# A recurrent layer's cell: the tanh of a sum against a sigmoid with a bias, and a reordered cell update

## The chip, the cores and the metric

The kernel runs on one core of one Trainium2 chip. The metric is the device time of one execution in microseconds, the median of several runs; lower is better. The kernel before takes 7336.98 us (median of 3 runs, 7319.33 to 7514.56).

## What is computed

The whole program is a small network over 1250 nodes: a graph layer with attention, a linear-attention mix, a recurrent layer, then a second graph layer, a second attention and two levels of experts. The change touches the recurrent layer alone. It walks over the 1250 nodes as over time steps, with 512 hidden values:

```python
def step(carry, x_t):
    h_prev, c_prev = carry
    combined = jnp.concatenate((x_t, h_prev), axis=1)
    f_t = jax.nn.sigmoid(combined @ W_f + b_f)
    i_t = jax.nn.sigmoid(combined @ W_i + b_i)
    c_tilde = jnp.tanh(combined @ W_c + b_c)
    c_t = f_t * c_prev + i_t * c_tilde
    o_t = jax.nn.sigmoid(combined @ W_o + b_o)
    h_t = o_t * jnp.tanh(c_t)
    return ((h_t, c_t), h_t)
```

Each step needs the hidden state of the step before it, so the 1250 steps are one chain.

## The kernel before, in words

The input's share of the gates is computed for all steps ahead of the loop. In the loop (`lstm`, two steps written out per turn, `par` 0 and 1) TensorE multiplies the hidden state with the recurrent weights. The state is kept in `hp` as two float16 columns, a high part (column 30) and a low part (column 31). The 512 hidden values are 4 columns of 128, and everything after the matmuls is done in two halves `q`: half 0 is columns 0 and 1, half 1 is columns 2 and 3.

TensorE's `rows(par, q, k)` are 16 matmuls of 128 columns: the share of state column `k` in the gates of half `q`. A step has eight of them, 128 matmuls. The first three (48 matmuls) need only state columns 0 and 1 and start at `s_h[0]`. Then TensorE waits for `s_h[1]`, and two more `rows` (32 matmuls) finish the gates of half 0; the last three finish those of half 1. 12 matmuls into `spare` follow, which nothing reads.

VectorE turns the gates of a half to columns (`to_columns`, L1495) and sums the three parts of each (`add_up`, L1501, into `z`). ScalarE takes one tanh over all eight numbers of a half (L1461, into `th`), the gates' sigmoids being written as tanh of half their argument. Column 0 of `th` holds twice the cell. VectorE then forms the two products of the cell (`cell_terms`, L1507, into `terms`: twice the input part, and four times the forget part), opens the output gate (`open_gate`, L1512, into `go`) and sums the cell (`cell_sum`, L1518, back to column 0 of `th`). ScalarE takes the tanh of the cell (L1466, into `tc`), both columns of a half in one instruction. VectorE multiplies it with `go`: once to the float16 high part (`high`, L1525), once to `full` (L1526); `low` (L1531) writes their difference and releases TensorE through `s_h[q]`. ScalarE lays the next step's input (L1454) and keeps the hidden state (L1470) between.

Each engine works through its own list in the order in which it is written here; only semaphores tie them together. The order of a step on VectorE is written out by hand in `step`.

Of the kernel before, what the change touches and what calls it, by code (L numbers as in the profile page):

```python
# [11 lines left out]
ALU = mybir.AluOpType  # L12
ACT = mybir.ActivationFunctionType
# [1298 lines left out]
def lstm(g, d, x, h):  # L1312
# [7 lines left out]
    with ExitStack() as s0:  # L1320
        def sb(name, shape, dt=F32, scope=s0):
            return scope.enter_context(nc.sbuf_tensor(name, shape, dt))
# [3 lines left out]
        scale = sb("l_scale", [P, 2])  # L1326
        h_scale = sb("l_h_scale", [P, 2])
        with ExitStack() as s1:
# [11 lines left out]
            with nc.Block() as block:  # L1340
                @block.gpsimd
                def _(pool):
                    pool.partition_all_reduce(top[:, 1:2], top[:, 0:1], P, RMAX)
# [36 lines left out]
        with ExitStack() as s1:  # L1380
            wx = sb("l_wx", [P, KC, GATES * C], scope=s1)
            bias = sb("l_bias", [P, M16], scope=s1)
# [10 lines left out]
        hp = sb("l_hp", [P, 2, KC, 2 * SPREAD], F16)  # L1393
        turn = sb("l_turn", [P, 2, 2, GATES, 2 * SPREAD])
        z = sb("l_z", [P, 2, 8])
        th = sb("l_th", [P, KC, GATES + 1])
        terms = sb("l_terms", [P, KC, 2])
        go = sb("l_go", [P, KC])
        tc = sb("l_tc", [P, KC])
        full = sb("l_full", [P, 2, KC])  # L1400
        half_h = sb("l_half_h", [P, 2])
# [4 lines left out]
        def pair(name):  # L1406
            return [s0.enter_context(g.semaphore(f"l_{name}{q}")) for q in range(2)]

        s_gates, s_turned, s_sum, s_tanh, s_terms, s_open, s_cell, s_tcell, s_full, s_h = [
            pair(n) for n in ("gates", "turned", "sum", "tanh", "terms", "open", "cell", "tcell", "full", "h")]  # L1410
# [37 lines left out]

        @block.scalar
        def _(act):  # L1450
            act.preload_act_table(ACT.Tanh)

            def lay_input(t, par):
                act.activation(turn[:, par, :, :, 0:34:33].rearrange("p q g v -> p q v g"),  # L1454
                               xp[:, bass.ds(t, 1), :].rearrange("p a (q v g) -> p (a q) v g", q=2, v=2),
                               ACT.Copy).then_inc(s_input, 1)

            def step(t, par):
                for q in range(2):
                    act.wait_ge(s_sum[q], t + 1)  # L1460
                    act.activation(th[:, 2 * q:2 * q + 2, 1:],  # L1461
                                   z[:, q, :].rearrange("p (j m) -> p j m", m=GATES), ACT.Tanh,
                                   scale=2.0 ** -Z_BITS).then_inc(s_tanh[q], 1)
                for q in range(2):
                    act.wait_ge(s_cell[q], t + 1)
                    act.activation(tc[:, 2 * q:2 * q + 2], th[:, 2 * q:2 * q + 2, 0], ACT.Tanh,  # L1466
                                   scale=0.5).then_inc(s_tcell[q], 1)
                lay_input(t + 1, 1 - par)
                act.wait_ge(s_full[1], t + 1)
                act.activation(h[:, :, bass.ds(t, 1)].rearrange("p j a -> p (j a)"), full[:, par, :],  # L1470
                               ACT.Copy).then_inc(s_kept, 1)
            act.wait_ge(s_clean, 1)
            lay_input(0, 0)
            with act.Fori(0, N, 2) as t:
                step(t, 0)
                step(t + 1, 1)

        @block.vector
        def _(dve):
            for par in range(2):  # L1480
                for q in range(2):
                    dve.memset(banks[par][q][:, :], 0.0)
            for u in range(2):
                g.link(dve, dve.tensor_copy(half_h[:, u:u + 1], h_scale[:, 0:1]))
            g.link(dve, dve.memset(th[:, :, :], 0.0))
            dve.memset(turn[:, :, :, :, :], 0.0).then_inc(s_clean, 1)  # L1486
            g.link(dve, dve.memset(hp[:, 1, :, :], 0.0))
            dve.memset(hp[:, 0, 0:2, :], 0.0).then_inc(s_h[0], 1)
            dve.memset(hp[:, 0, 2:4, :], 0.0).then_inc(s_h[1], 1)

            def to_columns(t, par, q):
                dve.wait_ge(s_gates[q], t + 1)
                if q == 0:
                    dve.wait_ge(s_input, t + 1)
                dve.transpose(turn[:, par, q, :, 1:33],  # L1495
                              banks[par][q][:, 0:128].rearrange("p (m r) -> p m r", r=32)).then_inc(s_turned[q], 1)

            def add_up(t, par, q):
                dve.wait_ge(s_turned[q], t + 1)
                three = turn[:, par, q, :, :].rearrange("p g (v e) -> p v g e", e=SPREAD)[:, :, :, 0:3]  # L1500
                dve.tensor_reduce(z[:, q, :].rearrange("p (v g) -> p v g", g=GATES), three, AX.X,  # L1501
                                  ALU.add).then_inc(s_sum[q], 1)

            def cell_terms(t, q):
                two = slice(2 * q, 2 * q + 2)
                dve.wait_ge(s_tanh[q], t + 1)
                dve.scalar_tensor_tensor(terms[:, two, :], th[:, two, 1:3], 1.0, th[:, two, 0:GATES + 1:GATES],  # L1507
                                         ALU.add, ALU.mult).then_inc(s_terms[q], 1)

            def open_gate(t, q):  # L1510
                two = slice(2 * q, 2 * q + 2)
                dve.scalar_tensor_tensor(go[:, two], th[:, two, 3], 1.0, half_h[:, :], ALU.add,  # L1512
                                         ALU.mult).then_inc(s_open[q], 1)

            def cell_sum(t, q):
                two = slice(2 * q, 2 * q + 2)
                dve.wait_ge(s_terms[q], t + 1)
                dve.scalar_tensor_tensor(th[:, two, 0], terms[:, two, 0], 0.5, terms[:, two, 1], ALU.mult,  # L1518
                                         ALU.add).then_inc(s_cell[q], 1)

            def high(t, par, q):
                two = slice(2 * q, 2 * q + 2)
                dve.wait_ge(s_tcell[q], t + 1)
                dve.wait_ge(s_open[q], t + 1)
                dve.tensor_tensor(hp[:, 1 - par, two, 30], go[:, two], tc[:, two], ALU.mult)  # L1525
                dve.tensor_tensor(full[:, par, two], go[:, two], tc[:, two], ALU.mult).then_inc(s_full[q], 1)  # L1526

            def low(t, par, q):
                two = slice(2 * q, 2 * q + 2)
                dve.wait_ge(s_full[q], t + 1)  # L1530
                dve.tensor_tensor(hp[:, 1 - par, two, 31], full[:, par, two], hp[:, 1 - par, two, 30],  # L1531
                                  ALU.subtract).then_inc(s_h[q], 1)

            def step(t, par):
                to_columns(t, par, 0)
                add_up(t, par, 0)
                to_columns(t, par, 1)
                cell_terms(t, 0)
                open_gate(t, 0)
                add_up(t, par, 1)  # L1540
                cell_sum(t, 0)
                cell_terms(t, 1)
                high(t, par, 0)
                cell_sum(t, 1)
                low(t, par, 0)
                open_gate(t, 1)
                high(t, par, 1)
                low(t, par, 1)
            with dve.Fori(0, N, 2) as t:
                step(t, 0)  # L1550
                step(t + 1, 1)
            dve.wait_ge(s_h[1], N + 1)
            dve.wait_ge(s_kept, N)
            dve.scalar_tensor_tensor(x[:, :, 0:N], h[:, :, 0:N], h_scale[:, 1:2], x[:, :, 0:N], ALU.mult, ALU.add)
# [516 lines left out]
```

## Time and profile before

| | us |
|---|---|
| median of 3 runs | 7336.98 |
| profiled execution | 7332.33 |
| its span | 7330.6 |
| stretch of the recurrent loop (first to last `low` of the trace) | 1965.7 to 6229.5 |
| TensorE busy in the whole span | 5252.2 (72%) |
| VectorE busy | 3870.4 (53%) |
| ScalarE busy | 1844.6 (25%) |

The loop takes more than half of the span. The engines' shares over the whole span say little, since the parts outside the loop have other limits. In the loop the same pattern of instructions comes 1250 times, with the same gaps, so one step in the order of time tells what the others do. The columns of each view are named in the section of rows.

### The profile page before, as it was taken

The numbers are of one execution on the slowest core, as the hardware profiler recorded it, in microseconds if no ns is written. First come the engines' busy times: TensorE is split into PE (matmuls) and PEld (weight loads), VectorE is DVE, ScalarE is ACT, GpSimd is POOL, SyncE is SP. The second block draws the span as 40 slices with busy tenths as digits, with TensorE's granted clock in tenths as the row PEclk, the third lists the DMA queues.
The fourth block names the chain that finished last, engine by engine and source line by source line (L and its number), as shares of the span: only waits on it lengthen the run. The fifth ranks groups of instructions, "written<-read, shape, count | busy, mean of one in ns | idle before, by whom it ended". The sixth has DMA issues, their size and how long they took to land. (4 is left out here: it accounts for less than half of the span.)

```text
span 7330.6 us, 411790 instructions
## 1 busy us (share of the span) xinstructions
PE 5252.2 (72%) x180989; PEld 3541.9 (48%) x180989; DVE 3870.4 (53%) x22246; ACT 1844.6 (25%) x8790; POOL 875.2 (12%) x891
## 2 busy tenths in 40 slices
PE   1256354775977777777777777777777777877799
PEld 1122122442555555555555555555555555553445
DVE  6115355733466666666666666666666666573112
ACT  1001004820033333333333333333333333200011
POOL 0717563500000000000000000000000000350000
PEclk7677677987999999999999999999999999997899
DMA  2116465511000000000000000000000000230100
GB/s 71 40 70 200 138 175 100 159 37 46 0 0 0 0 0 0 0 0 0 0 0 0 0 0 0 0 0 0 0 0 0 0 0 0 86 80 23 46 0 15
DMA packets 116203, 235.83 MB, mean 32 GB/s; under 512 B 65390, under 2 KB 67054, under 8 KB 112251
## 3 DMA queue, kind: packets, MB, share of 16 engines
q0 software_dynamic: 56032, 162.48, 7.9%
q1 hardware_dynamic: 60058, 72.02, 3.2%
q8 instruction: 51, 0.84, 0.0%
q14 instruction: 62, 0.50, 0.0%
HBM read 219.99 MB, written 14.45 MB: 32 GB/s over the span
## 5 line engine op out<-in xcount | busy, mean ns | idle before, releaser
L1422 PE MATMUL l_bank<-l_w,l_hp 128*32 128x128 f16 x160000 | 2464.4, 219 | 998.7 <-DVE l_hp L1531 993.6
L1422 PEld LDWEIGHTS l_bank<-l_w,l_hp 128*32 128x32 f16 x160000 | 2246.3, 97 | 1633.0 <-DVE l_hp L1531 1627.4
L1495 DVE STREAM_TRANSPOSE l_turn<-l_bank 128x128 f32<-128x128 f32 x2500 | 794.5, 318 | 1180.0 <-PE l_bank L1422 1005.6
L1461 ACT ACTIVATE l_th<-l_z 128x8 f32<-128x8 f32 x2500 | 523.3, 209 | 2127.1 <-DVE l_z L1501 2127.1
L1443 PE MATMUL l_spare<-l_w 128*2 128x512 f16 x15000 | 1025.7, 379 | 0.0
L1674 POOL DMA_INDIRECT ga_rows<-r_table,dst_t x176 | 168.0, 955 | 4643.7 <-DMA r_table<-c_r 4516.4
L1466 ACT ACTIVATE l_tc<-l_th 128x2 f32<-128x2 f32 x2500 | 490.9, 196 | 464.3 <-DVE l_th L1518 464.3
L1507 DVE SCALAR_TENSOR_TENSOR l_terms<-l_th 128x4 f32<-128x4 f32 x2500 | 359.2, 144 | 256.1 <-ACT l_th L1461 256.1
L1525 DVE TENSOR_TENSOR l_hp<-l_go,l_tc 128x2 f16<-128x2 f32 x2500 | 422.0, 169 | 130.4
L1501 DVE TENSOR_REDUCE l_z<-l_turn 128x8 f32<-128x24 f32 x2500 | 447.2, 179 | 42.6
L1531 DVE TENSOR_TENSOR l_hp<-l_full,l_hp 128x2 f16<-128x2 f32 x2500 | 422.2, 169 | 43.2
L1518 DVE SCALAR_TENSOR_TENSOR l_th<-l_terms 128x2 f32<-128x2 f32 x2500 | 386.0, 154 | 0.0
L1526 DVE TENSOR_TENSOR l_full<-l_go,l_tc 128x2 f32<-128x2 f32 x2500 | 385.6, 154 | 0.0
L1512 DVE SCALAR_TENSOR_TENSOR l_go<-l_th,l_half_h 128x2 f32<-128x2 f32 x2500 | 381.6, 153 | 0.0
L1443 PEld LDWEIGHTS l_spare<-l_w 128*2 128x2 f16 x15000 | 304.6, 84 | 152.4
L1470 ACT ACTIVATE xn<-l_full 128x4 f32 x1250 | 262.3, 210 | 359.8 <-DVE l_full L1526 359.8
L1137 PE MATMUL at_bank<-at_rows,at_onehot 128*128 128x512 f32 x352 | 199.8, 650 | 124.5 <-ACT at_rows L1096 54.1
L1454 ACT ACTIVATE l_turn<-l_xp 128x16 f32 (+1 forms) x1251 | 275.0, 220 | 2.6 <-DVE l_turn L1486 2.6
L751 POOL DMA_INDIRECT sm_q_rows<-q_table,sorted_e x176 | 199.4, 1133 | 275.1 <-POOLq L117 140.1
L1960 PE MATMUL e_y<-e_hid,e_w 128*128 128x512 f32 (+1 forms) x576 | 222.1, 541 | 0.0
L913 DVE TENSOR_TENSOR sm_q_rows<-sm_q_rows,sm_k_rows 128x512 f32<-128x512 f32 x176 | 122.1, 694 | 187.7 <-DMA sm_k_rows<-k_table,sorted_e 179.5
L1989 DVE TENSOR_TENSOR e_masked<-e_h,e_m_all 128x512 f32<-128x512 f32 (+1 forms) x72 | 40.0, 597 | 324.5 <-PE e_h L1945 324.5
(413 smaller groups left out, 4896.0 us busy)
## 6 DMA issues: line engine op xcount, KB each, us to landing
keys<-in_src_by_tile SPq DMA_DIRECT2D x7, 1344.0 KB
e_w<-in_e_W SPq DMA_DIRECT2D x2, 4096.0 KB
w<-in_g_W SPq DMA_DIRECT2D x2, 2048.0 KB, 10.4
l_wh<-in_l_Wh SPq DMA_DIRECT2D x1, 4096.0 KB
l_wx<-in_l_Wx SPq DMA_DIRECT2D x1, 4096.0 KB
e_w<-in_e_W SPq DMA_DIRECT2D x2, 2048.0 KB
sm_q_rows<-q_table,sorted_e POOLq DMA_INDIRECT x176
sm_k_rows<-k_table,sorted_e POOLq DMA_INDIRECT x176
```

The lines of the kernel that those rows point to most:

```text
L1422: mm = pe.matmul(banks[par][q][32 * j:32 * j + 32, 0:128], hp[:, par, k, 30 - 30 * v:62 - 30 * v], w16[:, part, k, j, 256 * q + 128 * v:25 ...
L1443: pe.matmul(spare[32 * j:32 * j + 2, 0:512], w16[:, 0, k, j, 0:2], w16[:, 0, k, j, :], start=True, stop=True)
L1461: act.activation(th[:, 2 * q:2 * q + 2, 1:], z[:, q, :].rearrange("p (j m) -> p j m", m=GATES), ACT.Tanh, scale=2.0 ** -Z_BITS).then_inc(s ...
L1466: act.activation(tc[:, 2 * q:2 * q + 2], th[:, 2 * q:2 * q + 2, 0], ACT.Tanh, scale=0.5).then_inc(s_tcell[q], 1)
L1495: dve.transpose(turn[:, par, q, :, 1:33], banks[par][q][:, 0:128].rearrange("p (m r) -> p m r", r=32)).then_inc(s_turned[q], 1)
L1501: dve.tensor_reduce(z[:, q, :].rearrange("p (v g) -> p v g", g=GATES), three, AX.X, ALU.add).then_inc(s_sum[q], 1)
L1507: dve.scalar_tensor_tensor(terms[:, two, :], th[:, two, 1:3], 1.0, th[:, two, 0:GATES + 1:GATES], ALU.add, ALU.mult).then_inc(s_terms[q], 1)
L1512: dve.scalar_tensor_tensor(go[:, two], th[:, two, 3], 1.0, half_h[:, :], ALU.add, ALU.mult).then_inc(s_open[q], 1)
L1518: dve.scalar_tensor_tensor(th[:, two, 0], terms[:, two, 0], 0.5, terms[:, two, 1], ALU.mult, ALU.add).then_inc(s_cell[q], 1)
L1525: dve.tensor_tensor(hp[:, 1 - par, two, 30], go[:, two], tc[:, two], ALU.mult)
L1526: dve.tensor_tensor(full[:, par, two], go[:, two], tc[:, two], ALU.mult).then_inc(s_full[q], 1)
L1531: dve.tensor_tensor(hp[:, 1 - par, two, 31], full[:, par, two], hp[:, 1 - par, two, 30], ALU.subtract).then_inc(s_h[q], 1)
```

## The change

The cell's tanh is written as a sigmoid: tanh(c) = 2 (sigmoid(2c) - 0.5). ScalarE's activation computes a function of scale times the input plus a bias, and a bias can be a column of memory, one number per partition. So the sum of the two products moves into the activation: with `terms[:, j, 0]` as input, scale 0.5 and `terms[:, j, 1]` as bias, ScalarE needs no `cell_sum` ahead of it. The bias is one number per partition, so each of the four columns takes an instruction of its own; there were two instructions per step, one per half, and there are four. `high` now subtracts 0.5 in the same instruction that multiplies with `go` (`scalar_tensor_tensor` in place of `tensor_tensor`), and `half_h` is doubled once ahead of the loop. `cell_sum` stays, because the next step needs the cell, but nothing in the same step waits for it; instead `cell_terms` waits for `s_cell` of the step before. Two small memsets ahead of the loop give `s_cell` its first count. The table of functions that ScalarE loads ahead of the loop is asked for by Sigmoid instead of Tanh.

Two orders change. On ScalarE both tanh of the gates stood ahead of both tanh of the cell; now each half's cell operations stand right behind its gates. On VectorE `high(0)` goes ahead of `cell_terms(1)`, and `cell_sum(1)` goes behind `open_gate(1)`.

```diff
-            act.preload_act_table(ACT.Tanh)
+            act.preload_act_table(ACT.Sigmoid)
...
-                for q in range(2):
-                    act.wait_ge(s_cell[q], t + 1)
-                    act.activation(tc[:, 2 * q:2 * q + 2], th[:, 2 * q:2 * q + 2, 0], ACT.Tanh,
-                                   scale=0.5).then_inc(s_tcell[q], 1)
+                    act.wait_ge(s_terms[q], t + 1)
+                    for j in (2 * q, 2 * q + 1):
+                        ins = act.activation(tc[:, j:j + 1], terms[:, j, 0:1], ACT.Sigmoid, scale=0.5,
+                                             bias=terms[:, j, 1:2])
+                    ins.then_inc(s_tcell[q], 1)
...
-                g.link(dve, dve.tensor_copy(half_h[:, u:u + 1], h_scale[:, 0:1]))
+                g.link(dve, dve.tensor_scalar(half_h[:, u:u + 1], h_scale[:, 0:1], 2.0, None, ALU.mult))
...
+            for q in range(2):
+                dve.memset(th[:, 2 * q:2 * q + 2, 0], 0.0).then_inc(s_cell[q], 1)
...
                 dve.wait_ge(s_tanh[q], t + 1)
+                dve.wait_ge(s_cell[q], t + 1)
...
-                dve.tensor_tensor(hp[:, 1 - par, two, 30], go[:, two], tc[:, two], ALU.mult)
-                dve.tensor_tensor(full[:, par, two], go[:, two], tc[:, two], ALU.mult).then_inc(s_full[q], 1)
+                dve.scalar_tensor_tensor(hp[:, 1 - par, two, 30], tc[:, two], 0.5, go[:, two], ALU.subtract, ALU.mult)
+                dve.scalar_tensor_tensor(full[:, par, two], tc[:, two], 0.5, go[:, two], ALU.subtract,
+                                         ALU.mult).then_inc(s_full[q], 1)
...
                 cell_sum(t, 0)
+                high(t, par, 0)
                 cell_terms(t, 1)
-                high(t, par, 0)
-                cell_sum(t, 1)
                 low(t, par, 0)
                 open_gate(t, 1)
+                cell_sum(t, 1)
                 high(t, par, 1)
```

ScalarE's list for one step of the kernel before, from the gates of the loop's first step on; `l_th<-l_z` is the tanh of a half's gates, `l_tc<-l_th` that of its cell:

```order
L1461 ACTIVATE l_th<-l_z 128x2x4 x2
L1466 ACTIVATE l_tc<-l_th 128x2 x2
L1454 ISA
L1454 ACTIVATE l_turn<-l_xp 128x2x2x4
L1470 ISA
L1470 ACTIVATE xn<-l_full 128x4
```

The same step on ScalarE in the changed kernel:

```order
L1461 ACTIVATE l_th<-l_z 128x2x4
L1466 ACTIVATE l_tc<-l_terms 128x1 x2
L1461 ACTIVATE l_th<-l_z 128x2x4
L1466 ACTIVATE l_tc<-l_terms 128x1 x2
L1454 ISA
L1454 ACTIVATE l_turn<-l_xp 128x2x2x4
L1471 ISA
L1471 ACTIVATE xn<-l_full 128x4
```

The two instructions of half 0's cell now stand between the two tanh of the gates, each reads one column, and no load of another table stands in the loop.

VectorE's list before, from the second `add_up` of a step to its last `low`:

```order
L1501 TENSOR_REDUCE l_z<-l_turn 128x8
L1518 SCALAR_TENSOR_TENSOR l_th<-l_terms 128x2
L1507 SCALAR_TENSOR_TENSOR l_terms<-l_th 128x4
L1525 TENSOR_TENSOR l_hp<-l_go,l_tc 128x2
L1526 TENSOR_TENSOR l_full<-l_go,l_tc 128x2
L1518 SCALAR_TENSOR_TENSOR l_th<-l_terms 128x2
L1531 TENSOR_TENSOR l_hp<-l_full,l_hp 128x2
L1512 SCALAR_TENSOR_TENSOR l_go<-l_th,l_half_h 128x2
L1525 TENSOR_TENSOR l_hp<-l_go,l_tc 128x2
L1526 TENSOR_TENSOR l_full<-l_go,l_tc 128x2
L1531 TENSOR_TENSOR l_hp<-l_full,l_hp 128x2
```

And in the changed kernel, where each line number of these functions is 3 to 5 higher:

```order
L1504 TENSOR_REDUCE l_z<-l_turn 128x8
L1522 SCALAR_TENSOR_TENSOR l_th<-l_terms 128x2
L1529 SCALAR_TENSOR_TENSOR l_hp<-l_tc,l_go 128x2
L1530 SCALAR_TENSOR_TENSOR l_full<-l_tc,l_go 128x2
L1511 SCALAR_TENSOR_TENSOR l_terms<-l_th 128x4
L1536 TENSOR_TENSOR l_hp<-l_full,l_hp 128x2
L1516 SCALAR_TENSOR_TENSOR l_go<-l_th,l_half_h 128x2
L1522 SCALAR_TENSOR_TENSOR l_th<-l_terms 128x2
L1529 SCALAR_TENSOR_TENSOR l_hp<-l_tc,l_go 128x2
L1530 SCALAR_TENSOR_TENSOR l_full<-l_tc,l_go 128x2
L1536 TENSOR_TENSOR l_hp<-l_full,l_hp 128x2
```

`high` of half 0 (two instructions) has moved ahead of the second `cell_terms`, and the second `cell_sum` has moved behind `low(0)` and `open_gate(1)`. The list has as many instructions as before.

## Rows read from the trace of the kernel before

**Rows 1.** Busy time by stage: stretch, length, PE, PEld, DVE, ACT, POOL, PEclk, DMA share, GB/s.
```profile
3000.00:4000.00 1000.00, 767.03 (x41020) 582.60 (x41020) 613.17 (x4688) 308.88 (x1758) 0.00 (x0) 1.00 0.00 0
```

**Rows 2.** The line of `low`: count, ns min/median/max, first and last start.
```profile
L1531 DVE TENSOR_TENSOR l_hp<-l_full,l_hp x2500: 168/169/171, 1965.7 to 6229.5; 128x2 f16<-128x2 f32 x193
```

**Rows 3.** Timeline of one step: start us, duration us, engine, line, out<-in, [idle before].
```profile
4001.62 0.32 DVE L1495 STREAM_TRANSPOSE l_turn<-l_bank 128x128 f32<-128x128 f32 x1 [0.81 <-PE l_bank L1422]
4001.97 0.18 DVE L1501 TENSOR_REDUCE l_z<-l_turn 128x8 f32<-128x24 f32 x1
...
4002.18 0.21 ACT L1461 ACTIVATE l_th<-l_z 128x8 f32<-128x8 f32 x1 [1.24 <-DVE l_z L1501]
4002.29 0.32 DVE L1495 STREAM_TRANSPOSE l_turn<-l_bank 128x128 f32<-128x128 f32 x1
4002.53 0.12 DVE L1507 SCALAR_TENSOR_TENSOR l_terms<-l_th 128x4 f32<-128x4 f32 x1
...
4002.64 0.18 DVE L1501 TENSOR_REDUCE l_z<-l_turn 128x8 f32<-128x24 f32 x1
4002.74 0.15 DVE L1518 SCALAR_TENSOR_TENSOR l_th<-l_terms 128x2 f32<-128x2 f32 x1
4002.85 0.21 ACT L1461 ACTIVATE l_th<-l_z 128x8 f32<-128x8 f32 x1 [0.46 <-DVE l_z L1501]
4002.97 0.19 ACT L1466 ACTIVATE l_tc<-l_th 128x2 f32<-128x2 f32 x1
4003.09 0.16 DVE L1507 SCALAR_TENSOR_TENSOR l_terms<-l_th 128x4 f32<-128x4 f32 x1 [0.21 <-ACT l_th L1461]
4003.19 0.17 DVE L1525 TENSOR_TENSOR l_hp<-l_go,l_tc 128x2 f16<-128x2 f32 x1
4003.26 0.15 DVE L1526 TENSOR_TENSOR l_full<-l_go,l_tc 128x2 f32<-128x2 f32 x1
4003.34 0.16 DVE L1518 SCALAR_TENSOR_TENSOR l_th<-l_terms 128x2 f32<-128x2 f32 x1
4003.45 0.17 DVE L1531 TENSOR_TENSOR l_hp<-l_full,l_hp 128x2 f16<-128x2 f32 x1
4003.53 0.20 ACT L1466 ACTIVATE l_tc<-l_th 128x2 f32<-128x2 f32 x1 [0.37 <-DVE l_th L1518]
...
4003.68 1.79 PEld L1422 LDWEIGHTS l_bank<-l_w,l_hp 128*32 128x32 f16 x128 [1.30 <-DVE l_hp L1531]
4003.68 1.97 PE L1422 MATMUL l_bank<-l_w,l_hp 128*32 128x128 f16 x128 [0.80 <-DVE l_hp L1531]
4003.79 0.17 DVE L1525 TENSOR_TENSOR l_hp<-l_go,l_tc 128x2 f16<-128x2 f32 x1
...
4004.06 0.17 DVE L1531 TENSOR_TENSOR l_hp<-l_full,l_hp 128x2 f16<-128x2 f32 x1
...
4005.03 0.32 DVE L1495 STREAM_TRANSPOSE l_turn<-l_bank 128x128 f32<-128x128 f32 x1 [0.80 <-PE l_bank L1422]
```

**Rows 4.** Groups of ScalarE with an operand of one number per partition: count, busy, mean ns.
```profile
L1096 ACT ACTIVATE at_rows<-at_rows,weight_t 128x64 f32<-128x64 f32 x528 | 144.5, 336 | 24.9 <-DMA at_rows<-v_table,dst_t 21.3 <-issue 0.7
...
L1084 ACT ACTIVATE at_apart<-numbers_f,at_minus_lo 128x128 f32<-128x128 f32 x176 | 68.0, 386 | 41.6 <-DVE at_minus_lo L1104 41.3 <-PE at_bank L1138 0.3
```

**Rows 5.** Timeline of ScalarE: three such instructions back to back.
```profile
1300.25 0.81 ACT L1096 ACTIVATE at_rows<-at_rows,weight_t 128x64 f32<-128x64 f32 x3
```

**Rows 6.** Timeline of the loop's first step, in which TensorE has its lower clock.
```profile
1961.00 3.49 PE L1422 MATMUL l_bank<-l_w,l_hp 128*32 128x128 f16 x128 [5.19 <-DVE l_hp L1488]
1963.38 0.32 DVE L1495 STREAM_TRANSPOSE l_turn<-l_bank 128x128 f32<-128x128 f32 x1 [2.36 <-PE l_bank L1422]
```

**Rows 7.** Stretch of that first step, TensorE's gate matmuls (L1422) alone; columns as in the view by stage.
```profile
1961.00:1964.00 3.00, 3.00 (x116) 3.00 (x120) 0.50 0.00 0
```

**Rows 8.** Groups of ScalarE: the load of a function table.
```profile
L1451 ACT ACT_TABLE_LOAD x1 | 1.3, 1283 | 208.8 <-PEq L73 208.8
```

## The prediction, made before the changed kernel was run

> **What bounds the kernel now.** I read the busy time by stage first: in a stretch inside the recurrent loop TensorE is busy 77% of the time, VectorE 61%, ScalarE 31%, no DMA moves, and TensorE's granted clock is 1.00, which is 2.4 GHz [rows 1]. No engine is full, so a chain of latencies sets the time. The line of `low` gives the period: 2500 instructions, two per step, the first starting at 1965.7 and the last at 6229.5 us; 4263.8 us over 1249.5 steps is 3.41 us per step [rows 2]. 0.01 us per step is therefore 12.5 us of the kernel, and everything is decided in the timeline of one step [rows 3].
>
> I set the first transpose (half 0, 4001.62) to zero; the next comes at 4005.03, 3.41 later. In that chain an engine starts about 0.03 us after the one that releases it has ended (sum of half 1 ends 4002.82, its tanh starts 4002.85; `cell_sum(1)` ends 4003.50, its tanh starts 4003.53), and VectorE behind ScalarE takes 0.03 to 0.06 (tanh of the cell 1 ends at 4003.73, `high(1)` starts 4003.79) [rows 3].
>
> Two chains go round, one for each half of the state.
> - Half 0: sum, tanh of gates, terms, `cell_sum(0)` ends at 1.27, its tanh runs 1.35 to 1.54, `high`, `full`, `low(0)` 1.83 to 2.00, TensorE starts at 2.06. From there to the next transpose 1.35. Sum 3.41: this is the chain that binds.
> - Half 1: tanh of gates ends 1.44, `cell_terms(1)` 1.47, `cell_sum(1)` 1.72 to 1.88 (behind `high` and `full` of half 0 on VectorE, not at its earliest), tanh of the cell 1.91 to 2.11, `high(1)` 2.17, `low(1)` 2.44 to 2.61. Adding the same 0.06, TensorE can see it at 2.67.
>
> When does TensorE want half 1? Its 128 weight loads span 1.79 us, the last of them taking some 0.09, so they start 13.4 ns apart [rows 3]. The 49th, the first that needs half 1, starts 48 x 13.4 = 0.64 after 2.06, at 2.70. Half 1 is there at 2.67. **The second half is hidden by 0.03 us, no more.** That is the number to watch: whatever makes half 0 faster is capped there, and whatever makes half 1 later than 0.03 us is paid in full.
>
> The return of half 1 is shorter than that of half 0 only because 48 matmuls are done already: 1.35 - 0.64 = 0.71 from the 49th to the transpose. As a check, 2.67 + 0.71 = 3.38, against the 3.41 of half 0.
>
> **The change, part by part.**
>
> Removed from the path: `cell_sum` ahead of each tanh of the cell. In half 0 the terms end at 1.03 (4002.65) and the cell operation can start at 1.06, where the tanh of the cell started at 1.35: 0.29 earlier. (Of this, `cell_sum(0)` cost only 0.15; the rest was its place behind the second sum, and the tanh of half 1's gates on ScalarE.)
>
> Added: each cell operation is two instructions with a bias column. The old one took 0.19 to 0.20 for both columns [rows 3]. The loop has none with a column operand; the rest of the program has. 128x128 elements with a bias column take 386 ns, 128x64 with a scale column 336 [rows 4]. The 64 elements between them cost about 50, so a width of one leaves about 280 ns. Three of the 64-wide ones back to back take 0.81 us [rows 5]; (0.81 - 0.336) / 2 = 0.237 from start to start, less 0.05 for the width: 0.19. A pair then takes s = 0.19 + 0.28 = 0.47 us from first start to end, against 0.20: **+0.27 each, twice in a step**. The bounds: if the column cost nothing at this width, a pair takes 0.10 + 0.195 = 0.295 (0.12 from tanh start to tanh start at 8 elements [rows 3]); if the two did not overlap at all, 0.56. I take 0.47, because both forms of rows 4 give the same base of 280.
>
> Half 0 after: cell operation 1.06 to 1.53; `high(0)` 1.56, `full` 1.64, `low(0)` at about 1.83, where it was. The 0.29 gained by the missing sum and the earlier place are spent on 0.27 of longer pair and a little waiting: half 0 breaks even.
>
> Half 1 after: ScalarE is held by the pair until 1.44 (1.06 + 2 x 0.19), so the tanh of half 1's gates, ready at 1.23, runs 1.44 to 1.65 instead of 1.23 to 1.44. On VectorE `cell_terms(1)` now stands behind `high(0)` and `full`: 1.64 + 0.08 = 1.72 at the earliest, and 1.68 by the tanh. It sits exactly where `cell_sum(1)` was (1.72), so the delayed tanh costs nothing and the removed sum gains nothing: in half 1 `terms` has only taken its place. Then comes the long pair. In general, with s: pair 0 ends 1.06 + s; `high(0)` +0.03; `full` +0.075; `cell_terms(1)` +0.075, ends +0.155; pair 1 starts +0.03, ends +s; `high(1)` +0.06; `low(1)` +0.27, ends +0.17; TensorE +0.06; transpose +0.71. **Period = 2.70 + 2s.** With s = 0.47 that is 3.64, and +0.23 per step. The stall shows between the 48th and the 49th matmul.
>
> Costed at nothing: `scalar_tensor_tensor` for `tensor_tensor` (both kinds on 128x2 take 0.15 with a float32 result [rows 3], and I give the float16 one its old 0.17); `cell_sum(0)`, in VectorE's pause before `high(0)`; `cell_sum(1)` and `open_gate(1)`, in its pause before `high(1)`, now about 0.5 us long (uncovered they would be 0.15 each); the wait for `s_cell`, given a step before (queued behind it are `low(0)` and all that follows, so 0.03 for a second wait would be passed on: it is in the range). The input laid for the next step ends about 0.27 later than before, at some 2.8, against the transpose at 3.64. The three instructions ahead of the loop are a fraction of a microsecond.
>
> Sum: 1250 x 0.23 = 288 us on the profiled execution's 7332.33, which lies 5 us under the median of the runs: **7620 us**, 3.9% slower.
>
> A table of functions is also asked for by Sigmoid. One load takes 1283 ns [rows 8]. If each change between tanh and sigmoid needed one, a step would take four, 5.1 us or more, some 6400 us in all. The changed program's list shows none inside the loop, so I leave this out. The Trainium skill (ScalarE: Activation LUTs, Table sets) says that functions come in sets and that sigmoid's set has tanh too. By that there is nothing to pay either; before a run no row shows it.
>
> **The rivals.**
> - The column costs little on a width of one (s = 0.295). Then the period is 3.29 by the formula, and half 0 gives 2.93 + s (1.06, +0.03 to `high`, +0.26 and +0.17 through `low`, +0.06, +1.35), 3.23. Saving 0.12 x 1250 = 150: 7180 us. For it: no instruction this narrow with a column operand is in the trace. Against: two widths, one base. It decides below s = 0.355, where 2.70 + 2s is 3.41. The two-per-cent line towards slower (+147 us, 0.117 per step) is at s = 0.41. Chance 0.07.
> - Half 1 is hidden after all, since TensorE's loads run ahead of what I read, or the waits behind `high` are shorter. Half 0 sets the period, 3.41 to 3.45: 7332 to 7380 us, no change to be measured. Against: the check 3.38 against 3.41 leaves no room for 0.2. Chance 0.06.
> - TensorE's clock falls, as its pauses grow by 0.23 us per step. The first step ran at a granted clock of 0.50, 1.2 GHz [rows 7], and took 2.38 from its start to the transpose against 1.35 [rows 6]. +1.03 per step would be 8900 us. For it: that step followed 5 us of idle. Against: two pauses of 0.8 and 0.23 with matmuls between, and 12 spare ones. Chance 0.02.
> - A longer step, same mechanism: no overlap in the pair, s = 0.56, period 3.82, 7845 us. Chance 0.04, of which the range leaves out most.
>
> **How the numbers follow.** The forecast's mechanism (half 1 late by twice the longer pair, less the 0.29 gained and the 0.03 hidden) has 0.81; its own range is +0.17 to +0.30 per step (s from 0.44 to 0.49, and 0.02 to 0.03 of second waits), 7540 to 7710. Reaching towards the rivals on both sides, 7500 to 7730 for 8 in 10. A difference of 2% is about what a measurement of this kernel can tell. Faster by more than that needs s under 0.30: 0.04. Within it, the rest of the first two rivals and the low tail of the forecast: 0.10. Slower: 0.86.
>
> **What would show it.** The cell operations: 2500 become 5000, about 0.28 each, starts 0.19 apart. `cell_sum` ends nobody's wait; ScalarE's pause before the second cell operation is ended by `l_terms`. TensorE's 128 matmuls split into 48 and 80 with a pause of about 0.2 between, released by `low(1)`, while half 0's `low` comes, from the first transpose, no later than before. Period 3.64. I am wrong if the pair takes under 0.41, if the 48 and 80 stay one block, or if half 0's `low` has moved by more than 0.05 either way.

## The result, and the profile after

| | before | after |
|---|---|---|
| median of the runs, us | 7335.96 (4 runs) | 7578.09 (4 runs) |
| profiled execution, us | 7332.33 | 7561.06 |
| first and last `low` of the loop, us | 1965.7, 6229.5 | 1959.0, 6463.3 |
| one step (the difference over 1249.5) | 3.412 | 3.605 |

The changed kernel is slower: ratio 1.0335, 95% interval 1.0307 to 1.0362. One of the four runs of the kernel before took 7514.56 us, over 2% more than the other three, and the ratio leaves it out. One step became 0.193 us longer, and 1250 x 0.193 is 241 us; the medians differ by 242. Everything outside the loop is as it was (the profiled execution differs by 229, because its loop began 7 us earlier and what follows took 5 us less).

The two lines that answer to [rows 2] and [rows 1] in the trace of after: first the line of `low`, with the starts of its first and last instruction; then a stretch inside the loop, with busy time of PE, PEld, DVE, ACT, POOL, then the granted clock.

```profile
L1536 DVE TENSOR_TENSOR l_hp<-l_full,l_hp x2500: 168/168/170, 1959.0 to 6463.3; 128x2 f16<-128x2 f32 x193
```

```profile
3000.00:4000.00 1000.00, 776.51 (x38791) 553.86 (x38780) 573.05 (x4443) 444.55 (x2220) 0.00 (x0) 1.00 0.00 0
```

ScalarE went from 309 to 445 us busy in 1000, with the clock of TensorE at 1.00 as before. VectorE's share fell, since the same work is spread over a longer step. The groups of the page show the new instruction and what waits on it (busy, mean ns, then the idle time ahead of it):

```profile
L1466 ACT ACTIVATE l_tc<-l_terms 128x1 f32<-128x1 f32 x5000 | 1202.7, 287 | 707.3 <-DVE l_terms L1511 707.3
...
L1529 DVE SCALAR_TENSOR_TENSOR l_hp<-l_tc,l_go 128x2 f16<-128x2 f32 x2500 | 420.7, 168 | 740.2 <-ACT l_tc L1466 740.2
```

`high` (now L1529) waits 740 us in all for the cell operation, 0.30 per half. Before, the idle time ahead of `high` was 130 us with no such release named.

One step of after in the timeline, to be laid beside [rows 3]; the first transpose is at 4001.56:

```profile
4001.56 0.32 DVE L1498 STREAM_TRANSPOSE l_turn<-l_bank 128x128 f32<-128x128 f32 x1 [0.74 <-PE l_bank L1422]
...
4002.47 0.12 DVE L1511 SCALAR_TENSOR_TENSOR l_terms<-l_th 128x4 f32<-128x4 f32 x1
...
4002.63 0.48 ACT L1466 ACTIVATE l_tc<-l_terms 128x1 f32<-128x1 f32 x2 [0.29 <-DVE l_terms L1511]
...
4003.01 0.19 ACT L1461 ACTIVATE l_th<-l_z 128x8 f32<-128x8 f32 x1
4003.14 0.17 DVE L1529 SCALAR_TENSOR_TENSOR l_hp<-l_tc,l_go 128x2 f16<-128x2 f32 x1 [0.31 <-ACT l_tc L1466]
4003.22 0.16 DVE L1530 SCALAR_TENSOR_TENSOR l_full<-l_tc,l_go 128x2 f32<-128x2 f32 x1
4003.29 0.16 DVE L1511 SCALAR_TENSOR_TENSOR l_terms<-l_th 128x4 f32<-128x4 f32 x1
4003.41 0.17 DVE L1536 TENSOR_TENSOR l_hp<-l_full,l_hp 128x2 f16<-128x2 f32 x1
4003.48 0.48 ACT L1466 ACTIVATE l_tc<-l_terms 128x1 f32<-128x1 f32 x2 [0.27 <-DVE l_terms L1511]
...
4003.63 0.68 PEld L1422 LDWEIGHTS l_bank<-l_w,l_hp 128*32 128x32 f16 x48 [1.31 <-DVE l_hp L1536]
...
4003.99 0.17 DVE L1529 SCALAR_TENSOR_TENSOR l_hp<-l_tc,l_go 128x2 f16<-128x2 f32 x1 [0.28 <-ACT l_tc L1466]
...
4004.26 0.17 DVE L1536 TENSOR_TENSOR l_hp<-l_full,l_hp 128x2 f16<-128x2 f32 x1
...
4004.48 1.13 PEld L1422 LDWEIGHTS l_bank<-l_w,l_hp 128*32 128x32 f16 x80 [0.17 <-DVE l_hp L1536]
4005.16 0.32 DVE L1498 STREAM_TRANSPOSE l_turn<-l_bank 128x128 f32<-128x128 f32 x1 [0.74 <-PE l_bank L1422]
```

Two things are to be seen. `low` of half 0 starts 1.85 us after the first transpose, where it started 1.83 before: half 0 has won nothing and lost next to nothing. And TensorE's block of 128 weight loads has broken in two, 48 and 80, with a pause of 0.17 us that ends with `low` of half 1. Before, `low` of half 1 started at 2.44 from the first transpose; now it starts at 2.70.

### The profile page after: what moved, and what is told of

Its sections match the earlier page's. It is cut to its first block and busy times, and to the rows that moved or that the text cites. A ratio compares the mean times of both kernels' runs of the same rounds, so it can differ in the third digit from the quotient of the medians.

```text
span 7559.3 us, 416792 instructions
## 1 busy us (share of the span) xinstructions
PE 5488.1 (73%) x180989; PEld 3556.8 (47%) x180989; DVE 3835.5 (51%) x22248; ACT 2528.1 (33%) x11290; POOL 878.4 (12%) x891
## 5 line engine op out<-in xcount | busy, mean ns | idle before, releaser
L1422 PE MATMUL l_bank<-l_w,l_hp 128*32 128x128 f16 x160000 | 2694.0, 220 | 1009.5 <-DVE l_hp L1536 1003.6
L1422 PEld LDWEIGHTS l_bank<-l_w,l_hp 128*32 128x32 f16 x160000 | 2259.3, 97 | 1860.4 <-DVE l_hp L1536 1854.8
L1466 ACT ACTIVATE l_tc<-l_terms 128x1 f32<-128x1 f32 x5000 | 1202.7, 287 | 707.3 <-DVE l_terms L1511 707.3
L1461 ACT ACTIVATE l_th<-l_z 128x8 f32<-128x8 f32 x2500 | 504.1, 202 | 1469.3 <-DVE l_z L1504 1469.3
L1529 DVE SCALAR_TENSOR_TENSOR l_hp<-l_tc,l_go 128x2 f16<-128x2 f32 x2500 | 420.7, 168 | 740.2 <-ACT l_tc L1466 740.2
L1530 DVE SCALAR_TENSOR_TENSOR l_full<-l_tc,l_go 128x2 f32<-128x2 f32 x2500 | 384.7, 154 | 0.0
```

The lines of the kernel that those rows point to most:

```text
L1422: mm = pe.matmul(banks[par][q][32 * j:32 * j + 32, 0:128], hp[:, par, k, 30 - 30 * v:62 - 30 * v], w16[:, part, k, j, 256 * q + 128 * v:25 ...
L1461: act.activation(th[:, 2 * q:2 * q + 2, 1:], z[:, q, :].rearrange("p (j m) -> p j m", m=GATES), ACT.Tanh, scale=2.0 ** -Z_BITS).then_inc(s ...
L1466: ins = act.activation(tc[:, j:j + 1], terms[:, j, 0:1], ACT.Sigmoid, scale=0.5, bias=terms[:, j, 1:2])
L1529: dve.scalar_tensor_tensor(hp[:, 1 - par, two, 30], tc[:, two], 0.5, go[:, two], ALU.subtract, ALU.mult)
L1530: dve.scalar_tensor_tensor(full[:, par, two], tc[:, two], 0.5, go[:, two], ALU.subtract, ALU.mult).then_inc(s_full[q], 1)
```

## The experiments

In all of them I read the step's length from the first and last start of `low`. Five of them ran on two other chips, on which the kernel before takes 7128 and 7122 us (last column of the table); on the first of these, the four kernels and the one before were run once each. The loop begins there some 190 us sooner (`low` first starts at 1768.8 us with a third instruction in half 0, at 1959.0 in after), while the loop itself is no different as far as these runs show: with that third instruction the time is 478.5 us over before's on the same chip, and 1250 x (3.791 - 3.412) is 474. So the step is the measure, and times are compared with before on the same chip. Times in the steps' accounts are from the first transpose. "Pair" is the two instructions of a half's cell operation, and s is the time from its first start to its end: 0.48 us in after.

| kernel | step, us | against before | time, us | before there |
|---|---|---|---|---|
| before | 3.412 | | 7335.96 | |
| after | 3.605 | +0.193 | 7578.09 | 7335.96 |
| one instruction, no bias | 3.144 | -0.268 | 6803.73 | 7127.88 |
| two instructions, no bias | 3.235 | -0.177 | 6898.29 | 7127.88 |
| a third one in half 0 | 3.791 | +0.379 | 7606.42 | 7127.88 |
| a third one in half 1 | 3.792 | +0.380 | 7600.12 | 7127.88 |
| changed cell in half 0 only | 3.527 | +0.115 | 7485.68 | 7341.08 |
| changed cell in half 1 only | 3.412 | 0.000 | 7341.21 | 7341.08 |
| both orders alone | 3.556 | +0.144 | 7518.31 | 7341.08 |
| changed cell, old orders | 3.689 | +0.277 | 7472.48 | 7121.54 |
| after, TensorE's rows early | 3.585 | +0.173 | 7558.26 | 7341.08 |

### How long is the pair, and why

```diff
-                    for j in (2 * q, 2 * q + 1):
-                        ins = act.activation(tc[:, j:j + 1], terms[:, j, 0:1], ACT.Sigmoid, scale=0.5,
-                                             bias=terms[:, j, 1:2])
-                    ins.then_inc(s_tcell[q], 1)
+                    act.activation(tc[:, 2 * q:2 * q + 2], terms[:, 2 * q:2 * q + 2, 0], ACT.Sigmoid,
+                                   scale=0.5).then_inc(s_tcell[q], 1)
```

> The changed kernel, but each half's cell operation is one sigmoid over both columns of the first product, with no bias; the second product is left out of the sigmoid, so this kernel computes another hidden state. The pair (0.48 us from first start to end in the trace of after) becomes one instruction of about 0.20. Theory 1 (the length of the pair, once per half in one chain, is the whole price; after's own trace gives period = 2.64 + 2s): the formula gives 3.04, but then half 0 and TensorE's 48 matmuls set it, at about 3.15 us per step instead of 3.61, some 7000 us in all, faster than before too; TensorE's weight loads are one block of 128 again. Theory 2 (the new orders on ScalarE and VectorE, or the second waits, cost the time): the step stays above 3.41 us, 7330 us or more.

Measured: 3.144 us per step. The line of the cell operation and TensorE's loads in its trace:

```profile
L1465 ACT ACTIVATE l_tc<-l_terms x2500: 203/203/204, 1774.0 to 5702.0; 128x2 f32<-128x2 f32 x193
```

```profile
4004.10 1.80 PEld L1422 LDWEIGHTS l_bank<-l_w,l_hp 128*32 128x32 f16 x128 [1.03 <-DVE l_hp L1534]
```

With the same orders, the same second waits and the same instructions on VectorE, but an operation of 0.20 us instead of a pair of 0.48, the loop is 0.27 us per step shorter than before, and the block of loads is whole. So the new orders and the second waits don't keep the step above 3.41 once the pair is short, and theory 2 falls. The terms of half 0, which have one of the new waits, start 0.91 us after the first transpose in before and in after alike (4002.53 and 4002.47). What the orders cost where the sum stays is another matter, and is measured below.

```diff
-                        ins = act.activation(tc[:, j:j + 1], terms[:, j, 0:1], ACT.Sigmoid, scale=0.5,
-                                             bias=terms[:, j, 1:2])
+                        ins = act.activation(tc[:, j:j + 1], terms[:, j, 0:1], ACT.Sigmoid, scale=0.5)
```

> As the run before, but still two instructions per half, one per column, each without the bias column (the second product is left out of the sigmoid here too). This parts the price of a second instruction from that of the column operand. If the column operand is what makes the pair long (0.09 per instruction), a pair takes 0.30: period 3.24 us by the formula 2.64 + 2s, 7105 us. If it is the second instruction as such, whatever its operands, the pair stays near 0.48 and the kernel at 7560 us.

Measured: 3.235 us per step, and this line (count, ns min/median/max):

```profile
L1466 ACT ACTIVATE l_tc<-l_terms x5000: 186/195/203, 1762.7 to 5805.4; 128x1 f32<-128x1 f32 x193
```

```profile
4002.08 0.29 ACT L1466 ACTIVATE l_tc<-l_terms 128x1 f32<-128x1 f32 x2 [0.29 <-DVE l_terms L1510]
```

Without the column operand an instruction takes 195 ns, with it 287, both on one column; a pair takes 0.29 against 0.48. The second instruction costs 0.09 us and the two column operands together 0.19. The Trainium skill (ScalarE: Activation LUTs, What ACT_TABLE_LOAD costs) gives some 93 ns for each such operand and as much for the overlap of two activations in a row; the 92 ns here and the starts 0.19 apart agree.

### Are both pairs in the chain?

A third sigmoid with a bias column goes into a spare column, in half 0 or in half 1:

```diff
                     for j in (2 * q, 2 * q + 1):
+                        if j == 1:
+                            act.activation(tc[:, KC:KC + 1], terms[:, j - 1, 0:1], ACT.Sigmoid, scale=0.5,
+                                           bias=terms[:, j - 1, 1:2])
```

> The changed kernel with one more sigmoid with a bias column (into a spare column that nothing reads) between the two of half 0 only. The group of half 0 grows from 0.48 to 0.67 us. Theory 1 (half 0's pair delays half 1 through VectorE's order: high and full of half 0 stand ahead of the terms of half 1): +0.19 us per step, 3.80, 7800 us. Theory 2 (only half 1's pair is on the path, half 0 has slack while TensorE waits for half 1): no change, 7560 us.

> The same third instruction in half 1 only. Theory 1: also +0.19 us per step, 3.80, 7800 us, with TensorE's pause between its 48th and 49th weight load grown from 0.17 to 0.36. Theory 2, were half 0 the one that binds: less than that, the more so the more half 1 is covered.

Measured: 3.791 and 3.792, +0.186 and +0.187 over after, for 0.19 us more in one half. Of half 0 it is plain why in the trace: `high` goes from 1.58 to 1.77 (4002.20, the first transpose being at 4000.43), the terms of half 1 behind it from 1.73 to 1.92. In half 1 it shows in TensorE's pause between 48 and 80 loads, 0.36 us against 0.17:

```profile
4003.96 0.68 PEld L1422 LDWEIGHTS l_bank<-l_w,l_hp 128*32 128x32 f16 x48 [1.32 <-DVE l_hp L1539]
4005.00 1.13 PEld L1422 LDWEIGHTS l_bank<-l_w,l_hp 128*32 128x32 f16 x80 [0.36 <-DVE l_hp L1539]
```

So the step grows by s of each half, 2s in all, once half 1 is late. The slack of half 0 towards TensorE doesn't help: half 1's terms stand behind half 0's `high` in VectorE's list.

### One half at a time

The changed operation in half 0 only, with the changed orders, except that the sum of half 1 stands ahead of `open_gate(1)` and not behind it (half 1 keeps its sum and its one tanh; `half_h` has a value for each column):

```diff
+NEW = 0
...
+                if q == NEW:
+                    act.wait_ge(s_terms[q], t + 1)
+                    for j in (2 * q, 2 * q + 1):
+                        ins = act.activation(tc[:, j:j + 1], terms[:, j, 0:1], ACT.Sigmoid, scale=0.5,
+                                             bias=terms[:, j, 1:2])
+                    ins.then_inc(s_tcell[q], 1)
+                else:
+                    act.wait_ge(s_cell[q], t + 1)
+                    act.activation(tc[:, 2 * q:2 * q + 2], th[:, 2 * q:2 * q + 2, 0], ACT.Tanh,
+                                   scale=0.5).then_inc(s_tcell[q], 1)
```

> Half 0 has the changed cell operation and the changed orders; half 1 has the old one (cell sum, then one tanh over both columns), with its cell sum right behind low of half 0. Theory 1, worked out on after's timeline: terms of half 1 end at 1.89 from the first transpose, cell sum 1.93 to 2.08, tanh 2.11 to 2.31, high 2.35, low ends 2.79, TensorE 2.84, transpose at 3.52: +0.11 us per step against before, 7470 us, ratio 1.019 to before. Theory 2 (each pair costs its own 0.27, the sum it replaces is worth little): about half of the whole loss, 7450 us; the two are not told apart by this run but by the next.

Measured: 7485.68 us, ratio 1.020 (1.0183 to 1.0217), 3.527 us per step. As said there, this one alone decides nothing. The same with `NEW = 1`, and both orders as in the kernel before:

> Half 1 has the changed cell operation, half 0 the old one, and both engines' orders are those of before. Theory 1 (what matters is where the terms of half 1 stand): they can start at 1.47, behind the tanh of the gates and ahead of high of half 0, the pair runs 1.66 to 2.14, high of half 1 at 2.17 where it was before; half 0 still binds: 3.41 us per step, 7335 us, the same as before within 0.3%. Theory 2 (a pair costs 0.27 wherever it stands): +0.25 us per step, or at least half of the change's loss, 7450 us or more.

Measured: 7341.21 us, ratio 0.9997 (0.9987 to 1.0006), 3.412 us per step. The pair is in its trace, 0.48 us long, and costs nothing:

```profile
4002.00 0.16 DVE L1522 SCALAR_TENSOR_TENSOR l_terms<-l_th 128x4 f32<-128x4 f32 x1 [0.21 <-ACT l_th L1474]
4002.09 0.17 DVE L1546 TENSOR_TENSOR l_hp<-l_go,l_tc 128x2 f16<-128x2 f32 x1
...
4002.20 0.48 ACT L1463 ACTIVATE l_tc<-l_terms 128x1 f32<-128x1 f32 x2
...
4002.71 0.17 DVE L1541 SCALAR_TENSOR_TENSOR l_hp<-l_tc,l_go 128x2 f16<-128x2 f32 x1
```

The first transpose is at 4000.52 here. The terms of half 1 start at 1.48, ahead of half 0's `high`, the pair runs from 1.68 to 2.16, and half 1's `high` starts at 2.19, against 2.17 in the kernel before. The sum that was taken away stood late on VectorE, at 1.72 behind `high` and `full` [rows 3]; without it the pair starts 0.23 earlier and is 0.28 longer. A pair is not a loss in itself. It is one where it can't start earlier by about as much as it is longer.

### The orders alone, and the operation alone

The kernel before with the changed orders and nothing else:

```diff
-                for q in range(2):
                     act.wait_ge(s_cell[q], t + 1)
                     act.activation(tc[:, 2 * q:2 * q + 2], th[:, 2 * q:2 * q + 2, 0], ACT.Tanh,
                                    scale=0.5).then_inc(s_tcell[q], 1)
...
-                cell_terms(t, 1)
                 high(t, par, 0)
-                cell_sum(t, 1)
+                cell_terms(t, 1)
                 low(t, par, 0)
                 open_gate(t, 1)
+                cell_sum(t, 1)
```

> The kernel before with both orders of the change (ScalarE: each half's cell tanh behind its gates; VectorE: high of half 0 ahead of the terms of half 1, cell sum of half 1 behind open gate) and nothing else of it: the sum and the one tanh per half stay. Theory 1: half 1's terms wait until 1.68, its sum until 1.94, TensorE sees it at 2.85: 3.53 us per step, +0.12, 7480 us. A rival (the orders are harmless, the pair alone is the loss): 7335 us.

Measured: 7518.31 us, ratio 1.0237 (1.022 to 1.0254), +0.144 per step, 0.02 more than expected. Three lines of its timeline, the first transpose being at 4001.65: the terms of half 1 start at 1.69 (1.47 in before), its sum at 1.96 (1.72), its tanh at 2.14.

```profile
4003.34 0.16 DVE L1506 SCALAR_TENSOR_TENSOR l_terms<-l_th 128x4 f32<-128x4 f32 x1
...
4003.61 0.15 DVE L1517 SCALAR_TENSOR_TENSOR l_th<-l_terms 128x2 f32<-128x2 f32 x1
...
4003.79 0.20 ACT L1465 ACTIVATE l_tc<-l_th 128x2 f32<-128x2 f32 x1 [0.54 <-DVE l_th L1517]
```

And the changed operation in both halves with the old orders:

```diff
-                    act.wait_ge(s_terms[q], t + 1)
-                    for j in (2 * q, 2 * q + 1):
+                for q in range(2):
+                    act.wait_ge(s_terms[q], t + 1)
+                    for j in (2 * q, 2 * q + 1):
...
-                high(t, par, 0)
                 cell_terms(t, 1)
+                high(t, par, 0)
+                cell_sum(t, 1)
                 low(t, par, 0)
                 open_gate(t, 1)
-                cell_sum(t, 1)
```

> The other half of the cut made by the run of the orders alone: the new cell operation in both halves, with both engines' orders as before (both tanh of the gates ahead of both pairs; terms of half 1 ahead of high of half 0). The two pairs then follow each other on ScalarE: 1.35 to 1.83 and 1.73 to 2.21 from the first transpose, high of half 0 at 1.86, its low ends 2.29, TensorE 2.35, and half 0 binds: 3.70 us per step, +0.29 against before, 7700 us, ratio 1.049, with TensorE's loads in one block of 128 (half 1 follows 0.4 us behind half 0 and is hidden). If the losses simply add (both +0.193, orders alone +0.144), the operation alone would be +0.05, 7400 us.

Measured: 7472.48 us, ratio 1.0486 (1.0468 to 1.0503), 3.689 us per step, +0.277. ScalarE does its four instructions in one row, 0.84 us, and TensorE's loads are whole: half 0 binds here.

```profile
4000.26 0.84 ACT L1467 ACTIVATE l_tc<-l_terms 128x1 f32<-128x1 f32 x4
...
4000.76 0.17 DVE L1530 SCALAR_TENSOR_TENSOR l_hp<-l_tc,l_go 128x2 f16<-128x2 f32 x1 [0.21 <-ACT l_tc L1467]
...
4001.25 1.80 PEld L1422 LDWEIGHTS l_bank<-l_w,l_hp 128*32 128x32 f16 x128 [1.58 <-DVE l_hp L1537]
```

Orders alone +0.144, operation alone +0.277, both together +0.193: the parts don't add. With the old orders half 0's pair starts behind the second tanh of the gates and half 0 pays; with the new ones half 0 is even and half 1 pays. The new orders take 0.08 off what the new operation costs, but nothing off the kernel before.

### Filling the pause

```diff
                 rows(par, 1, 0, first=True)
+                rows(par, 1, 1)
                 pe.wait_ge(s_h[1], t + 1)
                 rows(par, 0, 2)
                 rows(par, 0, 3, signal=s_gates[0])
-                rows(par, 1, 1)
```

> The changed kernel, and TensorE does the 16 matmuls of state column 1 for half 1's gates ahead of its wait for half 1 of the state instead of behind half 0's gates. They fill the pause (0.85 us from half 0 to half 1, 64 matmuls take 0.86). Theory 1: the first transpose is not earlier for it, since half 1's arrival sets it, but the gates of half 1 are ready 0.21 us earlier, the second transpose no longer holds the terms of half 0 back (0.91 becomes about 0.81 from the first transpose): -0.09 us per step, 3.51, 7450 us. If the second transpose doesn't hold the terms: no change, 7560 to 7578 us.

Measured: 7558.26 us, 3.585 us per step, 0.02 less than after where I had expected 0.09. The mechanism is there but small, and it meets the next limit. From its timeline, the first transpose being at 4000.19:

```profile
4000.64 0.32 DVE L1498 STREAM_TRANSPOSE l_turn<-l_bank 128x128 f32<-128x128 f32 x1
4001.00 0.17 DVE L1511 SCALAR_TENSOR_TENSOR l_terms<-l_th 128x4 f32<-128x4 f32 x1
```

The second transpose comes at 0.45 instead of 0.67 and the terms start at 0.81 instead of 0.91. But here they take 0.17 us instead of 0.12, so they end only 0.05 earlier. Half 1's `low` starts at 2.65, as much earlier as that. And TensorE's pause is gone: it starts at 2.01, and 96 matmuls stand between that and the first transpose, 1.57 us, 0.22 more than the 1.35 of 80 [rows 3]. Half 0 binds again at 2.01 + 1.57 = 3.58, with half 1 right at its heels: `low(1)` ends at 2.82, and the load of the 65th matmul, the first that needs half 1, starts 0.855 after the first load, at 2.87, where it starts 0.852 behind the first in before.

No kernel that computes the whole layer was faster than the one before. The one without the second product (3.144) shows what a cheap sum inside the activation would be worth, not a way to it.

## Why the prediction was right, and where its sizes were off

It said 7620 us, range 7500 to 7730, slower; measured were 7578. By its own steps:

- **The chain and its slack.** Right. Half 1 was hidden by no more than 0.03: in the run with the pair in half 1 only it came 0.02 later and nothing moved, and in after it came 0.26 later (`low(1)` 2.44 to 2.70) and the step grew by 0.193. Of the 0.26, some 0.03 were hidden and 0.04 came back behind TensorE's pause (see the formula below).
- **The length of the pair.** Predicted 0.47 from instructions 64 and 128 wide, measured 0.48; 287 ns each against 280. The rows themselves gave 286 (336 less 50), which I had rounded down. The rival of a cheap column at a width of one is out: 195 ns without the column, 287 with it.
- **Half 0 breaks even.** Right: `low(0)` at 1.85 against 1.83.
- **Half 1's terms take the place of its sum.** Right: 1.73 against 1.72. The run with one half changed shows the other side: the loss hangs on this place, since the pair costs nothing when the terms come at 1.48.
- **The formula 2.70 + 2s.** The factor two is shown by the third instruction in either half, +0.19 each. The constant was too large. With s = 0.48 the formula gives 3.66, and measured was 3.605, so the constant is 2.645. Two of its terms had been taken from the kernel before, in which TensorE has no pause. `high(1)` started 0.03 us after the pair, not 0.06 (4003.96 to 4003.99). And from TensorE's restart to the transpose it took 0.68 us (4004.48 to 4005.16), not 0.71. I had taken the weight loads to start evenly, 13.4 ns apart, and subtracted 48 of them from 1.35. The starts of the single loads in the two traces show that they are not even: they come in fours, a four every 56 ns, which is 14.0 ns a load, but at the head of a row the second four starts 15 ns behind the first. After the pause that head start comes a second time. From the start of the 49th load to that of the 81st it is 0.447 us in before and 0.405 in after, and from the start of the 49th to the transpose 0.727 and 0.685 (medians over more than 1000 steps of each trace). These 0.06, less 0.02 for the longer pair, are the 0.04 us per step, some 45 us in all, between 3.64 and 3.605.
- **Costed at nothing.** Right as far as it can be read: the two instructions of `high` take 168 and 154 ns against 169 and 155, and the second wait did not move the terms of half 0. The input for the next step was laid by 2.52, not 2.8, in either case well ahead of the transpose.
- **The clock** stayed at 1.00. **The table of functions**: one load of 1283 ns ahead of the loop, as in [rows 8], and none in it, so sigmoid and tanh share one set here, as the Trainium skill (ScalarE: Activation LUTs, Table sets) has it.

## What to carry to other kernels

An operation that is taken off a chain is worth not its own duration but the distance to whatever stands ready next, in the data or in the engine's list: with the cell sum of 0.15 us off the path, and with the new orders, half 0's cell operation started 0.28 earlier (1.35 to 1.07), and half 1's no earlier at all (1.91 to 1.92). In half 0 neither did it alone: with the new orders and the sum it started 0.05 earlier (1.30), and with the sum off the path but the old orders not at all (1.35). Splitting one small activation into two with a column operand costs 0.28 us in place, so a bias that has to be per column pays only where at least that much is won ahead of it. Where two halves take turns, work out for each when its consumer wants it; with 0.03 us between them, a gain in half 0 is capped there, and a loss in half 1 is paid as soon as it exceeds them.

## What the hardware showed that I had not expected

- A pause in TensorE's row of weight loads gave 0.04 us of itself back, since the head start of the second four (above) came once more behind it. In the unbroken row of before the 49th load starts 0.628 us after the first and its matmul at 0.681; after the pause in after both start at 0.853. The 13.4 ns of the prediction are 128 loads with one such head start in them, 14.0 is the pace without it: in the run with the early rows 16 further matmuls ahead of the transpose took 0.22 us. I did not test what sets the head start.
- The same VectorE operation, the terms of half 0, was recorded at 0.12 us where it followed the transpose at once (starts 0.24 apart) and at 0.17 where it started 0.36 behind it. An earlier start of 0.10 us was therefore worth only 0.05. I did not test why.
